# Two cross attentions on one core: bias scaling, query loads by pairs, and turns, weights and banks at other places

## The reference

```
layer 1, for each batch b
q = Wq y + bq;  k = Wk y + bk;  v = Wv x + bv        8 heads of 16 rows
scores = q k^T / sqrt(128)  per head, over the 1024 columns;  att = softmax(scores)
o = Wo (att v) + bo + x
h = (o - mean(o)) * rsqrt(var(o) + 1e-5) * gn_w + gn_b         mean and var over the whole batch element
layer 2, hidden_states = h, traces = y, per batch 128 rows of 1024
lin(x, W, A, B) = x W + 2 x A B                       rank 16
q = lin(h, Wq..), 32 heads of 32;  k, v = lin(y, Wk..), lin(y, Wv..), 8 heads, each for 4 query heads
att = softmax(q k^T / sqrt(32));  out = h + lin(att v, Wo, Ao, Bo)
```

## Time and profile before

| | before |
|---|---|
| median of three runs | 1371.63 us |
| all three runs | 1376.06, 1371.63, 1371.59 |
| the profiled execution | 1379.2 us |
| its span | 1377.4 us |
| mean granted clock of TensorE in it | 0.994 |
| busy: PE / PEld | 1335.9 (97%) / 1052.0 (76%) |
| busy: DVE / ACT / POOL | 929.4 (67%) / 825.3 (60%) / 160.9 (12%) |
| DMA | 300.45 MB, mean 218 GB/s |

### The profile page before, as it was taken

How to read it: one execution, slowest core, us unless ns; L and a number is a source line. 1 busy time by engine, 2 the same in 40 slices (tenths; PEclk the granted TensorE clock), 3 DMA queues, 4 the chain that set the end, 5 groups by cost and what they waited for, 6 DMA issues and landing times.

```text
span 1377.4 us, 24115 instructions
## 1 busy us (share of the span) xinstructions
PE 1335.9 (97%) x7135; PEld 1052.0 (76%) x7135; DVE 929.4 (67%) x2075; ACT 825.3 (60%) x2924; POOL 160.9 (12%) x129
## 2 busy tenths in 40 slices
PE   6899999999999899999999999999999999999998
PEld 5777888888878788888888888767666676766666
DVE  5666666666665677777767776587676777666665
ACT  4466655555550677777757776676655566665441
POOL 6533333222210000000000000400000000000000
PEclk9999999999999999999999999999999999999999
DMA  7455556666655677777777777997989889897772
GB/s 187 148 180 190 191 188 193 218 218 218 227 175 179 199 217 234 231 224 228 219 233 228 219 223 246 284 257 226 248 243 264 243 251 248 237 256 228 226 222 77
DMA packets 198915, 300.45 MB, mean 218 GB/s; under 512 B 30658, under 2 KB 97828, under 8 KB 198276
## 3 DMA queue, kind: packets, MB, share of 16 engines
q1 hardware_dynamic: 198788, 298.92, 73.1%
HBM read 213.88 MB, written 84.93 MB: 217 GB/s over the span
## 4 chain that ended last, share of the span: by engine, by line
PE 84%; ACT 7%; DVE 3%; issue 3%; DMA 2%; SPq 1%; ACTq 0%; DVEq 0%
PE bank L660 24%; PE bank L697 21%; PE bank L556 11%; PE bank L715 7%; PE bank L748 5%; PE bank L759 4%; ACT lora_aT_kv L901 2%; PE bank L501 2%; PE bank L631 2%; ACT x_hi L893 1%; DMA q_stack<-lse_dram 1%; ACT kv_sb L936 1%; PE bank L581 1%; PE bank L586 1%; PE bank L646 1%
## 5 line engine op out<-in xcount | busy, mean ns | idle before, releaser
L962 ACT ACTIVATE bank<-bank,negs 128x128 f32<-128x128 f32 x1024 | 349.5, 344 | 202.9 <-DVE negs L1216 202.6
L660 PE MATMUL bank<-hT,wq 128*128 128x512 f32 x1488 | 392.8, 401 | 3.1 <-DVE hT L1176 3.1
L697 PE MATMUL bank<-wo,op 128*128 128x512 f32 x1344 | 347.3, 396 | 2.9 <-DVE h_blk L1300 2.0
L660 PEld LDWEIGHTS bank<-hT,wq 128*128 128x128 f32 x1488 | 264.9, 189 | 50.4 <-DVE hT L1176 4.1
L697 PEld LDWEIGHTS bank<-wo,op 128*128 128x128 f32 x1344 | 250.1, 189 | 55.2 <-DVE op L1271 2.4
L1211 DVE TENSOR_REDUCE maxes<-bank 128x4 f32<-128x512 f32 x256 | 175.6, 686 | 127.1 <-PE bank L715 122.4
L979 ACT ACTIVATE probT<-bank 128x512 f32<-128x512 f32 x256 | 151.8, 605 | 107.0 <-PE bank L748 103.1
L962 ACT ACTIVATION_READ_ACCUMULATOR bank<-bank,negs 128x1 f32 x1024 | 212.8, 208 | 0.0
L556 PE MATMUL bank<-wkv_hi,yT 128*128 128x512 f32 x512 | 204.9, 421 | 0.3 <-POOL wkv_lo L1486 0.3
L715 PEld LDWEIGHTS bank<-k_stack,q_stack 96*128 96x128 f32 x1024 | 151.1, 192 | 20.7 <-DMA k_stack<-k_dram 5.0
L715 PE MATMUL bank<-k_stack,q_stack 96*128 96x128 f32 x1024 | 148.3, 268 | 4.2 <-DMA k_stack<-k_dram 3.9
(11 more groups left out here) (167 smaller groups left out, 1631.6 us busy)
## 6 DMA issues: line engine op xcount, KB each, us to landing
q_stack<-q_dram SPq DMA_DIRECT2D x384, 128.0 KB, 3.3
q_dram<-q_part SPq DMA_DIRECT2D x64, 512.0 KB, 4.5
q_stack<-q_dram SPq DMA_DIRECT2D x128, 256.0 KB, 3.7
y_in<-in_ctx SPq DMA_DIRECT2D x32, 512.0 KB, 4.5
x_in<-in_x SPq DMA_DIRECT2D x32, 512.0 KB, 5.2
h_dram<-h_out SPq DMA_DIRECT2D x32, 512.0 KB, 2.6
h_in<-h_dram SPq DMA_DIRECT2D x32, 512.0 KB, 4.5
k_stack<-k_dram SPq DMA_DIRECT2D x128, 128.0 KB, 3.2
```

The costliest lines, as they stand in the source:

```text
L660: m = pe.matmul(bank(u % 2).rearrange("p (a n) -> p a n", a=2), wq[:, block, part, c, :], hT[(group + 1) % 2][:, :, of, c, :], start=c == ...
L697: mm = pe.matmul(out_bank(pair, m), op[m][:, of, c, :], wo[m][w][:, c, :], start=c == 0 and of == 0 and w == 0, stop=c == GROUP - 1 and of ...
L962: act.activation(part, part, ACT.Exp, bias=negs[:, n % RING, j:j + 1], scale=SCORE1, accum_out=sums[:, score_column(k), g, j:j + 1]).then_ ...
```

## The change

1. ACT in layer 1: sum_y no longer scales the bias; a new scale_bias does, and it stands behind the copy of the mixed gram.
2. Between the layers: the first four turned tiles of h go to banks 0 and 1 in turn; mean and variance products of the last batch, with what follows them on DVE and ACT, stand one slot later.
3. turn_at: the tiles of all groups but the first are turned one slot sooner.
4. The first scores' queries are loaded for two units by one pair of DMAs, which the second scores' loads already did; four semaphores take the place of eight; a pair is loaded when both its places are free. The log rows stand ahead of keys and queries in SP's slot.
5. The upper parts of the output weights are made by halves on ACT.
6. In the last pair of blocks the products 3 to 6 go to banks 4 to 7.

The diff, with most of the lines around it left out:

```diff
@@ -222,7 +222,7 @@
             "h_in0", "h_in1", "hT_mm", "hT_hi", "hT_lo", "q_mm", "q_hi", "q_lo", "q_out0", "q_out1",
-            *(f"score_in{i}" for i in range(8)),
+            *(f"score_in{i}" for i in range(4)),
             "score_keys0", "score_keys1", *(f"again_in{i}" for i in range(4)), "rows_in0", "rows_in1", "v_in0", "v_in1", "sc_mm", "max", "neg", "exp",
...
@@ -361,11 +361,11 @@
         turn_at = {i - 4: i for i in range(4, 8)}
-        turn_at |= {12 + 2 * i: 8 + i for i in range(8)}
-        turn_at |= {4 * NC * (g - 1) + 4 * i + 2: 8 * g + i for g in range(2, NG) for i in range(8)}
+        turn_at |= {11 + 2 * i: 8 + i for i in range(8)}
+        turn_at |= {4 * NC * (g - 1) + 4 * i + 1: 8 * g + i for g in range(2, NG) for i in range(8)}
         def turn_bank(i):
-            return 3 if i < 4 else 2 + i % 2 if i < 8 else 2
+            return i % 2 if i < 4 else 2 + i % 2 if i < 8 else 2
...
@@ -395,7 +395,10 @@
         def out_bank(pair, m):
+            if pair == PAIRS - 1 and m > 2:
+                return bank(m + 1)
             return bank(2 if m in (0, 4) else (m in (2, 5)) ^ (pair % 2))
...
@@ -408,14 +411,14 @@
         for n in range(SCORE_UNITS):
-            score_place[n] = n % 8 if score_slot[n] < FIRST_STACK_LAST else n % GROUP
+            score_place[n] = n % 8 if score_slot[n - n % 2] < FIRST_STACK_LAST else n % GROUP
             place_freed[n] = last_in.get(score_place[n], -1) + 1
             last_in[score_place[n]] = n
-        TWO_STACKS = sum(w < FIRST_STACK_LAST for w in score_slot.values())
+        TWO_STACKS = sum(score_slot[n - n % 2] < FIRST_STACK_LAST for n in score_slot)
-            return 2 * DMA * (sum(score_place[e] == score_place[n] for e in range(n)) + 1)
+            return 2 * DMA * (sum(score_place[e] == score_place[n] for e in range(0, n, 2)) + 1)
...
@@ -427,7 +430,10 @@
         WO_LOADS = {QUERY_SLOTS + w: i for i, w in enumerate((-31, -28, -23, -18))}
-        WO_PARTS = {QUERY_SLOTS + w: m for m, w in enumerate((-24, -10, -6, -2, 2, 4, 6))}
+        WO_UPPER = {}
+        for m, halves in enumerate(((-24, -23), (-11, -10), (-7, -6), (-3, -2), (1, 3), (4, 5), (7, 8))):
+            for half, w in enumerate(halves):
+                WO_UPPER.setdefault(QUERY_SLOTS + w, []).append((m, half))
         WO_LOWER = {}
...
@@ -436,10 +442,10 @@
         soonest = 0
-        for n in range(SCORE_UNITS):
+        for n in range(0, SCORE_UNITS, 2):
             soonest = max(soonest, 8 * queries_out(score_half(n)) + 12)
-            if place_freed[n]:
-                soonest = max(soonest, score_slot[place_freed[n] - 1] + 1)
+            if place_freed[n + 1]:
+                soonest = max(soonest, score_slot[place_freed[n + 1] - 1] + 1)
             score_load_at.setdefault(soonest, []).append(n)
...
@@ -621,6 +627,9 @@
                     pe.wait_ge(S["hT_lo"], turn_freed[i])
+                elif i < 2:
+                    pe.wait_ge(S["yT_lo"], 2 * B)
                 elif turn_bank(i) == 3:
...
@@ -686,6 +695,11 @@
                             pe.wait_ge(S["q_lo"], NC * NG)
+                    elif pair == PAIRS - 1:
+                        if m < 5:
+                            pe.wait_ge(S["st_exp"], HALVES * GQ)
+                        else:
+                            pe.wait_ge(S["exp"], GQ * SCORE_UNITS)
                     elif m == 3:
...
@@ -708,7 +722,8 @@
                     pe.wait_ge(S[f"score_keys{k % 2}"], 2 * DMA * (k // 2 + 1))
-                pe.wait_ge(S[f"score_in{place}"], place_in(n))
+                if n % 2 == 0:
+                    pe.wait_ge(S[f"score_in{place // 2}"], place_in(n))
                 if score_freed[n]:
...
@@ -825,9 +840,9 @@
                     turn_h(turn_at[w])
-                if w == 0:
+                if w == 1:
                     mean_product(B - 1)
-                if w == 1:
+                if w == 2:
                     var_product(B - 1)
...
@@ -863,15 +878,17 @@
-            def out_hi(m):
-
-                if m in (0, 1, 5):
-                    act.wait_ge(S[f"wo_in{(0, 3, 0, 0, 0, 2)[m]}"], DMA)
-                else:
-                    act.wait_ge(S["wo_mix"], {2: 3, 3: 1, 4: 2, 6: 4}[m])
-
-                act.wait_ge(S["q_mm"], NC * (NG - 1) + (1, 5, 6, 7, 8, 8, 8)[m])
-                act.copy(wo[m][0][:], wo_raw[m][:]).then_inc(S["wo_hi"], 1)
+            def out_hi(m, half):
+                of = slice(2 * half, 2 * half + 2)
+                if half == 0:
+                    if m in (0, 1, 5):
+                        act.wait_ge(S[f"wo_in{(0, 3, 0, 0, 0, 2)[m]}"], DMA)
+                    else:
+                        act.wait_ge(S["wo_mix"], {2: 3, 3: 1, 4: 2, 6: 4}[m])
+                    act.wait_ge(S["q_mm"], NC * (NG - 1) + (1, 5, 6, 7, 8, 8, 8)[m])
+                act.copy(wo[m][0][:, of, :], wo_raw[m][:, of, :]).then_inc(S["wo_hi"], 1)
...
@@ -900,6 +917,8 @@
                 act.wait_ge(S[f"y_in{b % 2}"], DMA * (b // 2 + 1))
                 act.activation(lora_aT["kv"][:], y_in[b % 2][:], ACT.Copy,
                                accum_out=y_sum[:, b % 2:b % 2 + 1]).then_inc(S["ysum"], 1)
+
+            def scale_bias(b):
                 if b:
                     act.wait_ge(S["s_mm"], b)
                 act.wait_ge(S["ysum"], b + 1)
...
@@ -1015,6 +1034,7 @@
                 split_x(b)
                 if b:
                     begin_gram(b)
+                scale_bias(b)
                 if b and units_of(b - 1) and units_of(b - 1)[-1] < FIRST_O:
                     prep_round(units_of(b - 1)[-1])
                 round_yT(b + 1, 0)
...
@@ -1052,10 +1072,10 @@
                     round_hT(turn_at[w - 1])
-                if w == 3:
+                if w == 4:
                     write_h(B - 1)
-                if w in WO_PARTS:
-                    out_hi(WO_PARTS[w])
+                for part in WO_UPPER.get(w, ()):
+                    out_hi(*part)
                 if w in log_at:
...
@@ -1243,7 +1263,7 @@
                     dve.wait_ge(S["wo_mix"], (1, 4, 4, 3, 2, 3, 4)[m])
-                    dve.wait_ge(S["wo_hi"], m + 1)
+                    dve.wait_ge(S["wo_hi"], 2 * (m + 1))
                 dve.tensor_tensor(wo[m][1][:, of, :], wo_raw[m][:, of, :], f32(wo[m][0][:, of, :]),
...
@@ -1410,11 +1430,11 @@
                     split_hT(turn_at[w - 1])
-                if w == 1:
+                if w == 2:
                     deviation(B - 1)
-                if w == 2:
+                if w == 3:
                     norm_factors(B - 1)
-                if w == 3:
+                if w == 4:
                     norm_scale(B - 1)
...
@@ -1661,6 +1681,13 @@
+            def load_stack(stack, k, g, done):
+                places = f32(stack[:, g:g + 2, :, :]).rearrange("r g j n -> r g (j n)")
+                rows = q_dram[k, g * HD:(g + 2) * HD].rearrange("(g d) a n -> g d a n", g=2)
+                sp.dma_start(places[BOTH_ROWS], rows.rearrange("g d a n -> (d a) g n")).then_inc(done, DMA)
+                sp.dma_start(places[THIRD_ROWS], rows[:, :, 0, :].rearrange("g d n -> d g n")).then_inc(done, DMA)
             def load_queries(n):
...
@@ -1669,15 +1696,11 @@
                     for i in range(2):
                         sp.wait_ge(S[f"wo_out{i}"], raw_out(N_UNITS - 2 + i))
                     sp.wait_ge(S["ysum"], B)
-                if place_freed[n]:
-                    sp.wait_ge(S["sc_mm"], place_freed[n])
+                if place_freed[n + 1]:
+                    sp.wait_ge(S["sc_mm"], place_freed[n + 1])
                 if g == 0:
                     wait_queries(k)
-                stack = f32(q_stack[score_place[n] // GQ][:, g, :, :]).rearrange("r j n -> r (j n)")
-                rows = q_dram[k, g * HD:(g + 1) * HD]
-                done = S[f"score_in{score_place[n]}"]
-                sp.dma_start(stack[BOTH_ROWS], rows.rearrange("d a n -> (d a) n")).then_inc(done, DMA)
-                sp.dma_start(stack[THIRD_ROWS], rows[:, 0, :]).then_inc(done, DMA)
+                load_stack(q_stack[score_place[n] // GQ], k, g, S[f"score_in{score_place[n] // 2}"])
             def load_again(n):
...
@@ -1689,11 +1712,7 @@
                     wait_queries(k)
-                stack = f32(again_stack(k)[:, g:g + 2, :, :]).rearrange("r g j n -> r g (j n)")
-                rows = q_dram[k, g * HD:(g + 2) * HD].rearrange("(g d) a n -> g d a n", g=2)
-                done = S[f"again_in{n // 2 % 4}"]
-                sp.dma_start(stack[BOTH_ROWS], rows.rearrange("g d a n -> (d a) g n")).then_inc(done, DMA)
-                sp.dma_start(stack[THIRD_ROWS], rows[:, :, 0, :].rearrange("g d n -> d g n")).then_inc(done, DMA)
+                load_stack(again_stack(k), k, g, S[f"again_in{n // 2 % 4}"])
...
@@ -1806,12 +1825,12 @@
                 chunk = log_chunk(w, LOG_OUT)
                 if chunk is not None:
                     put_log(chunk)
+                for k in again_rows_at.get(w, ()):
+                    load_rows(k)
```

(2 more changed lines are left out.)

## The result

The changed kernel took 1351.75 us (median of four, 1350.93 to 1354.27), the kernel before in the same comparison 1373.36: ratio 0.9844, 95% interval 0.9820 to 0.9868. That is 21.6 us less; forecast were 1351 and a range of 1344 to 1363. The profiled execution took 1352.2, 27.0 less than that of before; the terms of the prediction add up to 23.6 for it, so they are 3.4 short of what the two profiles show.

A forecast was written before the change was run, and what follows sets the result against it. PE, 84% of the chain of waits, was taken as the bound. Terms 6.4+6.6+2.8+2.6+1.1+0.4+0+3.7 = 23.6 off the 1371.6 median give 1348.0, or 1354.6 without the keys' stall; middle 1351 us, range 1344 to 1363.

The forecast's parts named there:

- The gram wait: Layer 1: s_bq moved from ahead of the mixed gram's copy gives 0.23 in 28 batches, 6.4 us, bounds 0 and 8.7.
- The keys' stall: Keys of units 8 to 11, late behind 26 DMAs in SP's queue: query pairs save 6.6 us, 3.9 wait, rest clock.
- hT: Four waits for split tiles at groups' beginnings: turning a slot sooner saves 4 x 0.70 = 2.8 us, bounds 2.2 and 2.8.
- Transition: Between the layers: two banks in turn and the product a slot later remove four waits, 2.6 us, bounds 1.5 and 3.2.
- a sign of being wrong: In the profile after: L715 waiting for q_stack by more than 0.5 us anywhere would show the prediction wrong.
- Weights' stretch and log rows: Output weights' loads: fifth hT wait and rows issued ahead of queries, 1.1 us; a second wait for rows, later, 0.4.
- The halves: Upper output weights by halves on ACT: DVE is as full, so 0 us; bounds 2.4 lost and 2.8 gained.
- The last pair: Last 90 products: other banks remove the 1.98 wait and the lower clock behind it, 3.7 us, bounds 2.0 and 4.0.
- (1): Rival: the waits move on, DVE's chain deciding the same moment; only 9.1 us left, 1362.5 us; chance 0.13.
- (2): Rival: near 920 one long wait for DVE's splits replaces three short ones and the clock falls, 1353.4 us; chance 0.09.
- (3): Rival: query pairs land late in the stretch of products, 30 waits of 1.5 us, 1396 us; chance 0.03.
- (4): Rival: moved keys and tiles wait for something else; only transition and last pair remain, 1365.3 us; chance 0.03.

The follow-up runs named there:

- the mean product behind t1: The changed kernel with PE's mean product put behind t1 and DVE's gram adds ahead of aggregate and mean; 1359.02 us, ratio 0.9896.
- upper weights whole: The changed kernel with ACT's upper parts of the output weights whole again at their old slots; 1349.58 us, ratio 0.9829.
- the second profile: The kernel before run once more without any edit, for another profile of the same code; 1375.35 us.
- DVE made 7.1 slower: The changed kernel with the lower parts of output weights 4 and 5 made by POOL, no longer by DVE; 1358.27 us, ratio 0.9894.
- the last pair's banks: The kernel before with only the last pair's products 3 to 6 in banks 4 to 7; 1371.21 us, ratio 0.9970.
- the tiles a slot sooner: The kernel before with only the tiles of h turned one slot sooner; 1368.74 us, ratio 0.9961.
- part 1 alone: The kernel before with only the bias scaled behind the mixed gram's copy on ACT; 1364.46 us, ratio 0.9917.
- the transition: The kernel before with only the first turned tiles in banks 0 and 1 and the last batch's mean and variance a slot later; 1369.21 us, ratio 0.9962.

## Why the prediction was right, and where not

- *The gram wait.* Right in mechanism: DVE is next, 0.23 a batch, and mixed_x to t1 at 3.20, though in 26 of the 28 batches. The term was mis-sized, 6.4 for 8.0: it priced one link and stopped. The step "So 0.22 to 0.23 a batch of the 0.31" left out what stands behind t1. DVE's waits for POOL's power (12 waits of 0.2 before, none after) go as well, and with them 0.13 to 0.15 in each of 12 batches. The kernel with the mean product behind t1 is the same link pulled the other way: 0.49 lost behind t1 for 0.27 gained ahead of it.
- *The keys' stall.* The cause was right, SP's queue: moving the keys alone took the stall away as the pairs did. Its size in a typical run was the open question. It is not "in or out of the median", as the prediction put it, but of any size between: six profiles with the old order have 6.6, 5.9, 3.7, 3.7, 2.3 and 0.6, in the mean 3.8. The prediction's middle took half of 6.6, so it was near for a reason that it did not give, and that is luck.
- *hT.* 3.1 for 2.8, and 1.2 for the fifth; each wait cost 0.77, not 0.70.
- *Transition.* 2.6 when alone, 2.4 in the full change; predicted 2.6. Unit 0, which the prediction put at 0, takes 0.6 of it back, and in the other kernels with the whole change between 0 and 1.1. The worst (upper weights whole) has a wait of the first scores for q_stack of 0.87, over the 0.5 that the prediction named as a sign of being wrong.
- *Weights' stretch and log rows.* Predicted 1.5 together, 3.6 between the two profiles, and this is the step that failed: "The rows are now issued ahead of 192 KB of queries" and "The second wait for rows, later" (0.4) took two waits of one execution for the kernel's own, and their cure for the rows' place. The second profile of the same kernel does not have them, and putting the rows back changes nothing. Of the 3.6, 1.2 is the hT wait, and some 2.4 was that one execution's. Over many executions the log rows may still have given about 1 us, since waits for them stand in six of seven profiles with single loads and in one of seven with pairs; but then the pairs gave it, not the order of issue, which the prediction counted in full. That a 16 KB load behind large ones lands late (8.46 once) no run here could turn into time.
- *The halves.* 0 as forecast and for the reason given, shown from three sides: whole casts cost nothing, product 4's split made sooner only moved the wait to probT, and DVE made 7.1 slower made PE 6.9 later.
- *The last pair.* 3.7 forecast, 3.9 measured; 0.9970 for the edit alone. Of the 3.9 the wait is 2.0 and the clock behind it 1.6 to 1.9. The clock's share is not there in each execution, in five profiles of seven.
- *The sum.* Typical sizes are 8.0 (layer 1), 2.4 less 0.4 (transition and unit 0), 3.8 (stall), 3.1 and 1.2 (hT), 1.0 (log rows) and 3.4 (last pair), together 22.5. Measured were 21.6, with an interval from 18.1 to 24.7. That the forecast came within 1 us is in part luck: its gain, 20.6, was 1.0 too small (layer 1 above all), and the median that it started from, 1371.63, was 1.7 below that of the comparison, 1373.36.
- *Rivals.* The waits did not move on in layer 1 (1). No long stall with a low clock formed near 900 (2): the granted clock was 1.00 from 884 to 908. No pair was late among the products (3). Every part but the halves and the rows' place, which gave nothing, had its effect (4).

## What to carry to other kernels

A wait that an engine caused came back in nearly every profile of this kernel to 0.1 us, so one profile prices it; what the clock does behind it needs more than one. A wait that a DMA caused is one draw of a margin, so price the margin (issue against use, and how long landings vary) and take a second profile before counting it. When a chain is relieved, follow every instruction behind the relieved one, not only the next that waits: the second gain of layer 1 and the whole loss of the mean product behind t1 stood one link on. Here a queue with half as many DMAs for the queries gained at several places (ratio 0.9951), and one urgent DMA moved ahead at one (0.9986).

## What the runs showed of the hardware

- The landing of the same 64 KB of keys varied from 3.7 to 6.0 us, in kernels with nearly the same traffic around it. In each of the six, three issues ahead of it were held for 0.8 to 1.75 us. All six have the queries by single loads and the keys in their old place:

| profile | issued ahead of unit 7 | landing | wait of unit 8 | clock behind it | stall in all |
|---|---|---|---|---|---|
| before | 0.1 | 6.0 | 3.92 | fell | 6.6 |
| the last pair's banks | 0.4 | 5.0 | 2.64 | fell | 5.9 |
| the second profile | 0.7 | 4.5 | 1.86 | fell | 3.7 |
| the tiles a slot sooner | 0.1 | 3.9 | 1.89 | fell | 3.7 |
| part 1 alone | 0.6 | 4.6 | 2.06 | stayed | 2.3 |
| the transition | 1.4 | 3.7 | 0.38 | stayed | 0.6 |

- With pairs the same DMA was issued 4.0 to 5.5 us ahead of unit 7 in the seven profiles (446.25 against 450.51 in the changed kernel), but took 5.1 to 6.8 us to land.
- The clock after a wait of nearly the same length can stay or fall. After 2.06 (part 1 alone) it stayed, after 1.86 (the second profile) it fell; the last pair's 1.98 did either; after 2.46 for log rows (part 1 alone, at 868) it stayed. The four microseconds behind the wait in part 1 alone:

```profile
456.00:460.00 4.00, 4.00 (x24) 3.39 (x23) 2.80 (x6) 3.32 (x19) 0.00 (x0) 1.00 0.79 251
```

and in the second profile of before:

```profile
464.00:468.00 4.00, 4.00 (x15) 3.45 (x16) 2.35 (x5) 1.50 (x8) 0.00 (x0) 0.58 0.65 198
```

- DVE and POOL exclude each other in some operations. Beside POOL's 128x1024 subtractions two DVE operations with two SBUF inputs, of 0.69 us each, took 2.69 and 2.76, a cast of 0.43 took 2.07 and L1239 1.52 for 0.17; each ended 0.03 to 0.56 us behind the end of a POOL operation. DVE's operations that read PSUM (L1234, 0.68) kept their length. The Trainium skill, "SBUF — State Buffer", section "SBUF: two separate sides", says so: the pair of ports that the two share is an exclusive lock for the whole instruction, for a DVE operation with two SBUF inputs or in a two-port mode. The rows agree, with 1.4 to 2.1 us a time; whether the cast and L1239, which have one SBUF input, ran in such a mode the trace does not show.
